# Transposes of x and h: from TensorE and ScalarE to transposing DMAs issued by SyncE

## The reference, cut to what matters

```python
xn = _layernorm(x, axis=-1)
s = _L0_attn_ref(xn, ...)          # causal convolution over l, 128 taps for each of 256 channels, plus xn * D
g = _silu(_L0_ffn_ref(xn, w_gate, w_up, w_down))
return x + s * g

# _L0_ffn_ref: fp4_linear quantises both operands in blocks of 16 along the last dim to the grid
# 0, .5, 1, 1.5, 2, 3, 4, 6 times (largest of the block)/6, and multiplies
gate = fp4_linear(x, w_gate); y = fp4_linear(x, w_up)      # 256 -> 704, each
h = jax.nn.silu(gate) * y
return fp4_linear(h, w_down)                               # 704 -> 256
```

## Time and profile before

| | |
|---|---|
| median of three executions | 586.62 us |
| the profiled execution | 586.48 us, of which its span is 584.7 us |
| TensorE matmuls, weight loads | 473.7 us (4956), 331.3 us (4956) |
| GpSimd | 198.4 us (302) |
| DMA | 70.80 MB in 101186 packets, 121 GB/s on average |

### The profile page before, as it was taken

The page is one execution under the profiler, slowest core; times in us unless marked ns, Lnnn a source line. Parts: engine busy times, 40 slices in busy tenths (PEclk is TensorE's granted clock), DMA queues, the critical chain, the costliest instruction groups (busy, mean ns, idle before and its releaser), DMA issues.

```text
span 584.7 us, 13233 instructions
## 1 busy us (share of the span) xinstructions
PE 473.7 (81%) x4956; PEld 331.3 (57%) x4956; DVE 544.3 (93%) x689; ACT 407.2 (70%) x568; POOL 198.4 (34%) x302
## 2 busy tenths in 40 slices
PE   0000356668999999999999999999999999998965
PEld 0000234225555567777777777777777777765654
DVE  6999999989999999999999999999999999998884
ACT  6972866889988876767676767676767666664552
POOL 1094000474555551111111111333333333137870
PEclk9999957989999999999999999999999999999998
DMA  5990012225222335353534353535354535339978
GB/s 173 349 281 1 1 36 90 91 27 163 91 91 91 109 83 159 102 146 108 149 105 142 112 147 103 144 111 146 104 143 114 144 107 148 110 59 154 172 104 132
DMA packets 101186, 70.80 MB, mean 121 GB/s; under 512 B 8848, under 2 KB 100752, under 8 KB 101008
## 3 DMA queue, kind: packets, MB, share of 16 engines
q1 hardware_dynamic: 93072, 61.94, 35.8%
q0 software_dynamic: 8064, 8.13, 9.5%
HBM read 61.28 MB, written 16.91 MB: 134 GB/s over the span
## 4 chain that ended last, share of the span: by engine, by line
PE 57%; DVE 24%; issue 9%; POOL 6%; ACT 3%; DMA 0%; SPq 0%; DVEq 0%; POOLq 0%; ACTq 0%
PE ps L1224 27%; PE ps L1242 10%; PE ps L1244 5%; PE ps L1233 5%; PE ps L1257 4%; PE ps L1261 4%; DVE wgu L944 4%; DVE work L857 2%; DVE sm L799 2%; POOL gbuf L516 2%; DVE work L883 2%; PE ps L1212 2%; DVE work L852 2%; DVE xh L919 1%; DVE xh L912 1%
## 5 line engine op out<-in xcount | busy, mean ns | idle before, releaser
L1224 PE MATMUL ps<-wgu,work 128*128 128x512 f16 (+1 forms) x1152 | 242.7, 366 | 17.1 <-DVE work L883 15.9
L1224 PEld LDWEIGHTS ps<-wgu,work 128*128 128x128 f16 x1152 | 109.9, 99 | 128.0 <-issue 17.5
L615 ACT ACTIVATE work<-ps,con 128x704 f32<-128x704 f32 x64 | 54.2, 847 | 95.1 <-PE ps L1224 95.0
L1242 PE MATMUL ps<-wdh,work 128*128 128x256 f16 x704 | 87.9, 274 | 5.5 <-ACT gbuf L619 4.7
L610 ACT COPY work<-ps 128x1408 f16<-128x1408 f16 x64 | 84.7, 1325 | 2.1 <-PE ps L1233 1.9
L852 DVE SCALAR_TENSOR_TENSOR work<-work 128x960 f32<-128x960 bf16 (+2 forms) x67 | 71.8, 1110 | 1.6 <-ACT work L630 1.5
L1242 PEld LDWEIGHTS ps<-wdh,work 128*128 128x128 f16 x704 | 65.4, 98 | 13.4 <-issue 5.3
L516 POOL TENSOR_TENSOR gbuf<-gbuf,xh 128x256 f32<-128x256 f32 (+1 forms) x42 | 41.0, 1048 | 92.0 <-DVE work L865 77.8
L857 DVE SCALAR_TENSOR_TENSOR work<-work 128x1920 f16<-128x1920 bf16 (+3 forms) x36 | 69.7, 1936 | 1.2
L818 DVE TENSOR_TENSOR work<-work,ps 128x960 f32<-128x960 f32 (+2 forms) x63 | 68.4, 1126 | 1.1
L630 ACT ACTIVATE work<-work 128x960 bf16<-128x960 f32 (+2 forms) x67 | 61.8, 960 | 9.3 <-DVE work L818 8.7
(11 more groups left out here) (153 smaller groups left out, 675.1 us busy)
## 6 DMA issues: line engine op xcount, KB each, us to landing
work<-kpad SPq DMA_DIRECT2D x64, 512.0 KB, 3.8
work<-L_attn_u SPq DMA_DIRECT2D x33, 256.0 KB, 3.0
gbuf<-u_rev SPq DMA_DIRECT2D x4, 2048.0 KB, 18.6
out<-gbuf POOLq DMA_DIRECT2D x7, 1024.0 KB, 9.5
out<-L_attn_u SPq DMA_DIRECT2D x1, 768.0 KB, 5.5
out<-gbuf POOLq DMA_DIRECT2D x1, 768.0 KB, 8.1
work<-L_ffn_w_down SPq DMA_DIRECT2D x1, 704.0 KB, 6.6
work<-L_ffn_w_gate SPq DMA_DIRECT2D x1, 640.0 KB, 4.7
```

The source lines that it names most:

```text
L1224: last = T.matmul(p_gu[:, a:b], xT[par][:, t, c, :], wgu[:, part, c % 2, a:b], start=(n == 0), stop=(n == len(todo) - 1))
L1242: T.matmul(dst, hT[t][:, c, :], wdh[:, c, :], start=(c == 0), stop=False)
```

## The change

The 256 + 682 transposes of TensorE for x and for all h tiles but the last two, and ScalarE's copies of them, are gone. In their place SyncE issues `dma_start_transpose` from SBUF to SBUF: one for each pair of x (128 x 1024 f16, 256 KB) and one for each tile of h (128 x 1408 f16, 352 KB). The last two tiles keep the old way. SyncE's queue is written out step by step without a loop: in each step x of pair it+1, then the even tile of h, then `load_x`, then the first `load_t`, then the odd tile of h, then the other `load_t`s. `load_x` stood first before.

```diff
+            def x_transpose(p):
+                sp.wait_ge(x_hl, p * 2 + 2)
+                after(sp, gu_p, p * 2 - 2)
+                sp.dma_start_transpose(xT[p % 2].rearrange("p t c k -> p (t c) k"),
+                                       xhl[p % 2].rearrange("p t c -> p (t c)")).then_inc(x_td[p % 2], 16)
+            def h_transpose(n):
+                sp.wait_ge(hl_v, n // 2 + 1)
+                after(sp, dn_p, n - 1)
+                sp.dma_start_transpose(hT[n % 2], hilo[n // 2 % 2][:, n % 2, :]).then_inc(h_td[n % 2], 16)
+            x_transpose(0)
+            sp.wait_ge(k_all, 1)
+            x_transpose(1)
+            for it in range(NP + 1):
+                if 1 <= it < NP - 1:
+                    x_transpose(it + 1)
+                if it >= 2:
+                    h_transpose(it * 2 - 4)
+                if it < NP - 3:
+                    load_x(it + 3, (it + 1) % 2)
+                if it == 2:
+                    store_filter()
+                if it < S_CONV:
+                    copy_input(it)
+                if it == S_CONV:
+                    load_t(1, 1)
+                tiles = [n for n in range(2 * groups_before(it) + 2, 2 * groups_before(it + 1) + 2) if n < H // 4]
+                for n in tiles[:1]:
+                    load_t(n, n % 2)
+                if it >= 2:
+                    h_transpose(it * 2 - 3)
+                for n in tiles[1:]:
+                    load_t(n, n % 2)
...
 # ScalarE: x_copy gone, h_copy only for the last two tiles. VectorE: x_parts and h_parts
 # wait for the DMAs that read the buffers. TensorE:
             def gate_up(m, t, par, first):
                 if first is not None:
-                    pe.wait_ge(x_tc, first)
+                    pe.wait_ge(x_td[par], (first + 1 - par) * 8)
...
             def down(n, t, dst=None):
-                pe.wait_ge(hT_a, n + 1)
+                pe.wait_ge(*((h_td[t], (n - t) * 8 + 16) if n < NT - 2 else (hT_a, n - (NT - 3))))
...
-                if td:
-                    pe.wait_ge(hl_v, it - 1)
-                    h_transpose(it * 2 - 4, 0, par, copied=min(it + 1, NP))
-                if x:
-                    x_transpose(it + 1, 1 - par)
-                if td:
-                    h_transpose(it * 2 - 3, 1, par, copied=it + 2 if x else None)
```

More of the change, by code:

```diff
@@ L145, in build @@
         rs_p, fl_p = (ps[:, 3584 + NC * i:3584 + NC * i + NC] for i in range(2))
-        p_xT = ps[:, 1536:2048].bitcast(F16).rearrange("p (t c k) -> p t c k", t=2, c=4)
         yv = xh[:, :, :, :, :].rearrange("p q a t c -> p (q a t c)").bitcast(F32).rearrange(
@@ L216, in build @@
         x_hl = sem("x_hl")
-        x_tp = sem("x_tp")
-        x_tc = sem("x_tc")
+        x_td = [sem(f"x_td{i}") for i in range(2)]
+        h_td = [sem(f"h_td{i}") for i in range(2)]
         t_in = [sem(f"t_in{i}") for i in range(2)]
@@ L424, in copy_input @@
                 sp.dma_start(out[i:i + 1, 0:rows], u[i:i + 1, 0:rows]).then_inc(o_in, 16)
-            for it in range(PEEL):
-                load_x(it + 3, (it + 1) % 2)
+            def x_transpose(p):
[7 more added lines that the diff above has]
+                sp.dma_start_transpose(hT[n % 2], hilo[n // 2 % 2][:, n % 2, :]).then_inc(h_td[n % 2], 16)
@@ L428, in _ @@
+            x_transpose(0)
[8 more added lines that the diff above has]
+                    load_x(it + 3, (it + 1) % 2)
                 if it == 2:
                     store_filter()
[L430 to L447, removed]
-                    load_t(n, n % 2)
@@ L449, in _ @@
-            for n in range(2 * groups_before(NP - 3) + 2, H // 4):
-                load_t(n, n % 2)
+                if it < S_CONV:
[4 more added lines that the diff above has]
+                for n in tiles[:1]:
+                    load_t(n, n % 2)
+                if it >= 2:
+                    h_transpose(it * 2 - 3)
@@ L451, in _ @@
+                for n in tiles[1:]:
+                    load_t(n, n % 2)
+                if it == S_CONV - 1:
+                    sp.wait_ge(k_pad, 32)
+                    sp.wait_ge(k_dram, 16 * 16)
+                    sp.wait_ge(w_ca, 13)
+                    load_t(0, 0)
             for n in range(2):
@@ L600, in x_norm @@
                 ins.then_inc(x_n, 1)
[L602 to L605, removed]
             def h_copy(n, par, src=p_hT):
-                act.wait_ge(hT_p, n + 1)
-                after(act, dn_p, n - 1)
+                act.wait_ge(hT_p, n - (NT - 3))
+                act.wait_ge(dn_p, n - 1)
                 nc.scalar.copy(hT[par], src).then_inc(hT_a, 1)
@@ L643, in y_copy, with step @@
                                      scale=con[:, C_CONV:C_CONV + 1]).then_inc(cv_e, 1)
-            def step(it, par, x, xt, xn, gu, ch, td, a2=False, cv=0, c0=None, td1=True, first=True):
-                if td:
-                    h_copy(it * 2 - 4, 0)
+            def step(it, par, x, xn, gu, ch, td, a2=False, cv=0, c0=None, td1=True, first=True):
                 if a2 and first:
@@ L659, in step @@
                     silu_out(it * 2 - 5, 1, 1 - par)
-                if xt:
-                    x_copy(it + 1, 1 - par)
                 if cv:
@@ L667, in step @@
                     silu_gate(it * 2 + 1)
-                if td:
-                    h_copy(it * 2 - 3, 1)
                 if a2:
@@ L738, in _ @@
             weights_out(range(6, 8))
-            x_copy(0, 0)
             act.wait_ge(w_g, 3)
@@ L748, in _ @@
             weights_out(range(11, 13))
-            x_copy(1, 1)
             for it in range(PEEL):
-                step(it, it % 2, True, it >= 1, True, True, it >= 1, it >= 2, a2=True, td1=it >= 3, first=it >= 1)
+                step(it, it % 2, True, True, True, it >= 1, it >= 2, a2=True, td1=it >= 3, first=it >= 1)
                 if it == 1:
@@ L756, in _ @@
                 for par in range(2):
-                    step(q * 2 + (PEEL + par), par, True, True, True, True, True, True, a2=True)
+                    step(q * 2 + (PEEL + par), par, True, True, True, True, True, a2=True)
             act.wait_ge(con_ok, 1)
@@ L760, in _ @@
                 for par in range(2):
-                    step(q * 2 + (S_CONV + par), par, True, True, True, True, True, True, cv=2 - par, c0=q * 3 + 2 * par)
+                    step(q * 2 + (S_CONV + par), par, True, True, True, True, True, cv=2 - par, c0=q * 3 + 2 * par)
             for it in range(S_TAIL, NP - 2):
[L763 to L766, removed]
+                step(it, it % 2, True, it < NP - 3, True, True, True, cv=groups_of(it), c0=groups_before(it))
+            step(NP - 2, 0, False, False, True, True, True)
+            step(NP - 1, 1, False, False, True, True, True)
+            step(NP, 0, False, False, False, True, True)
             silu_out(NT - 3, 1, 0)
@@ L861, in x_parts @@
                 dve.wait_ge(x_r, p + 1)
-                after(dve, x_tp, p - 1)
+                after(dve, x_td[par], (p - par) * 8)
                 for part, scale in enumerate((shi, slo)):
@@ L886, in h_parts @@
                 own.settle()
-                after(dve, hT_p, p * 2 - 2)
+                after(dve, h_td[0], p * 16 - 16)
+                after(dve, h_td[1], p * 16 - 16)
                 t0, t1 = only[0], only[-1] + 1
@@ L1226, in gate_up, with h_transpose @@
                 last.then_inc(gu_p, 1)
[L1228 to L1231, removed]
+            def h_transpose(n, t, par, dst):
                 for c in range(NC11):
@@ L1262, in conv, with step @@
                 last.then_inc(cv_h, 1)
-            def step(it, par, x, gu, td, cv=0):
-                if td:
-                    pe.wait_ge(hl_v, it - 1)
-                    h_transpose(it * 2 - 4, 0, par, copied=min(it + 1, NP))
+            def step(it, par, gu, td, cv=0):
                 if gu:
                     gate_up(it * 2, 0, par, it + 1)
-                if x:
-                    x_transpose(it + 1, 1 - par)
                 if cv:
@@ L1288, in step @@
                     conv(groups_before(it) + 1, 1)
-            x_transpose(0, 0)
             pe.wait_ge(w_ca, 8)
@@ L1305, in _ @@
             transposed_down(4)
-            x_transpose(1, 1)
             gate_up(1, 1, 0, None)
@@ L1309, in _ @@
             for it in range(1, NP - 1):
-                step(it, it % 2, True, True, it >= 2, groups_of(it) if it >= S_CONV else 0)
-            step(NP - 1, 1, False, True, True)
-            step(NP, 0, False, False, True)
+                step(it, it % 2, True, it >= 2, groups_of(it) if it >= S_CONV else 0)
+            step(NP - 1, 1, True, True)
+            step(NP, 0, False, True)
             down(NT - 3, 1)
```

## The result

The changed kernel takes 614.48 us (median of 4 runs, 612.14 to 616.2) against 587.18 us for the kernel before in the same runs. The ratio is 1.0455, with a 95% interval of 1.0432 to 1.0478: slower by 27 us, where 580 was forecast. The profiled execution took 613.09 us with a span of 611.2.

What follows compares the result with a forecast made beforehand. VectorE's own 14.34 us was taken to bound the steps, with TensorE adding 0.61 us to every second one in the convolution stage. 586.5 - 6.1 - 1.5 + 1.0 = 579.9, say 580 us; range 575 to 650.

Steps and rivals of the forecast that it cites:

- The bound of the convolution stage: Convolution stage: TensorE adds 0.61 us to every second step; removing it saves 6.1 us, then VectorE's 14.34 us bounds.
- rival C: Whole kernel: nothing measurable, gain offset by a costlier start and TensorE's lower clock, 585 to 588 us; chance 0.13.
- The 0.8 us of `h_parts`' waits: VectorE: waits of `h_parts` for the transposes that free its buffer, 0.8 us in all, counted as gone.
- SyncE's issuing: SyncE's queue: each transposing DMA takes 1 to 2.5 us to issue, at most 9.0 of 14.34 us a step.
- Rival A: SyncE's queue: transposing DMAs worked off block by block become the bound, about 850 us at 0.72 a block; chance 0.24.
- The engines' time: DMA engines: transposes add 3.3 us a step by bytes, or 7.1 by packets; the first was taken.
- what hides them is the pipeline's slack: Each step: each h tile has about 13 us to land, about three times the 3.8 us in which 512 KB land.
- Rival B: Convolution stage: the filter's loads come late, 1 to 2 us lost in all 20 steps, 600 to 620 us; chance 0.20.
- The prediction's own sign of being wrong: Whole kernel: the prediction is wrong at its root if a transposing DMA takes over 5 us.
- The start: Before the first `gate_up`: x of pair 0 takes 3.0 to 4.5 us in place of 2.3; 1.0 us loss taken.
- the convolution's end: Where the convolution ends: the last `y_copy` comes earlier relative to VectorE by 0 to 2 us; 0.7 us gain taken.

Runs made afterwards that it cites:

- x_only: The changed kernel with x alone by transposing DMA, in all steps, and h on TensorE: 581.53 us, ratio 0.9905 to the kernel before.
- no_acc: The changed kernel with GpSimd's accumulating DMAs left out except the last one: 588.61 us, ratio 1.0005 to the kernel before.
- plain: The changed kernel with each transposing DMA replaced by a plain DMA of the same bytes in rows of 2816 or 2048 bytes: 587.21 us, ratio 0.9999.
- plain256: The changed kernel with each transposing DMA replaced by a plain DMA of as many bytes in pieces of 256 bytes: 594.55 us, ratio 1.0124.
- conv_even: The changed kernel with only the even h tile of steps 8 to 27 by transposing DMA, all else on TensorE: 582.10 us, ratio 0.9908.

## Why the prediction was wrong

**The bound of the convolution stage** was right. 0.61 us for two steps was TensorE's, VectorE's 14.34 came next, and x_only gets 6.0 of 6.1 us. In the changed kernel 0.4 arrived. The change itself took nearly all the rest: five steps longer by 0.82 us, from a clock that falls behind the gaps it opened, 4.1 us, and 0.06 us a step of VectorE, 1.3, with the second wait in front of `h_parts`. I had put the clock in rival C, in the steps before this stage. The 0.8 us of `h_parts`' waits that I counted as gone did not come: it waits 0.8 us in all for transposing DMAs up to 520 us.

**SyncE's issuing** was right, at the lower end: 1.24 us for x in the median and from 1.27 for h, whose median of 1.82 has waits in it, against 1 to 2.5 forecast. Rival A, work by the block in order, did not happen: 11 blocks landed in 4.5 us in the median. The 1309 ns for one block that the Trainium skill gives ("VectorE: DVE Perf Modes", The three transpose paths) thus does not multiply by blocks. The estimate of 2.3 us of issuing for h, from the push command for each tile in "DMA: Bandwidth & Descriptors" of the Trainium skill, is above the 1.27 measured.

**The engines' time** was mis-sized. I took 3.3 us a step, by bytes, and kept 7.1, by packets of 256 bytes at 29.4 ns. The runs show the second: 31 ns a packet. That transposing DMAs are as fast as regular ones ("Advanced Engine Details and Errata", X-Bar Transpose, in the Trainium skill) is not borne out here. Against plain ones of the same bytes in long rows the engines' share in two steps was 96.5% to 64.1%, against plain pieces of 256 bytes a packet took 31 to 23 ns, and beside accumulating DMAs 60 to 20.

**The step that failed** is "what hides them is the pipeline's slack": 13 us for each h tile, "about three times the 3.8 us". The 3.8 us was the landing time of plain loads in the convolution stage, used for a stretch in which GpSimd's DMAs keep the engines 0.94 full. There a transposing DMA took 19.1 us, and the slack was gone. Rival B looked at these steps and dismissed them by tile 60 and its wait of 4.08 us. The late tiles were those before it, first of all in step 31, with 9.68 us. As this stretch comes last, nothing behind it could make up for it: 20.9 of the 26.6 us, and with either kind of DMA left out the same stretch took 63.6 to 66.7 us, so it takes both. The prediction's own sign of being wrong, a transposing DMA of over 5 us, would not have shown this as a median over the run, which is 4.4.

**Near rival B by luck.** The 614.48 us lie in its 600 to 620, but not for its reasons. B wanted late loads of the filter in even steps and 1 to 2 us lost in each of 20 steps. TensorE's waits for these loads are 1.3 us in all and the stage is no longer than before.

**The odd tile of step 2** was a second use of the same slack: the order of SyncE's queue in that step puts 10.4 us of issuing in front of it, which stood in the earlier trace rows as 11.52. It costs 4.7 us.

**The start** was right in kind: the first `gate_up` begins at 89.05 us in place of 87.30, but step 1 only 0.2 later, for 1.0 forecast. That is one execution: of the eight kernels whose profiled execution has x of pair 0 by DMA, three have step 1 at 109.1 to 109.2 and five at 110.1 to 110.6, where the granted clock stayed at 0.50 for longer and the 18 products of the first `gate_up` took 6.2 us and more in place of 5.2 to 5.5. At the convolution's end step 29 is 0.6 us shorter, for 0.7 forecast, and by the forecast's mechanism: the last `y_copy` comes 0.46 us behind VectorE's first instruction of the step in place of 1.20.

## What to carry to other kernels

Price a DMA that is to replace compute in each stage by what else is on the DMA engines there, in packets and not bytes, and above all in the last stage, where lateness is not made up. Move only as much work off an engine as brings it under the next bound: here x alone, one set of transposes of three, is worth the whole gain, and all three cost the clock and the engines' room. If a change opens gaps on TensorE, look at the granted clock of the products behind them: here it fell behind gaps of 1.97 us in four steps and not behind one of 1.98. And read landing times by stage, since a median over the run can hide the stage that matters.

## What the runs showed of the hardware

- Transposing DMAs and accumulating DMAs of GpSimd slow each other: 3.5 us of landing for the one alone (no_acc), 10.5 for the other alone, 19.1 and 24.0 together, with fewer bytes moved in 28 us (4.1 MB) than by the accumulating ones alone (4.5). Plain pieces of the same size leave the latter at 11.5.
- Plain DMAs of 352 KB from SBUF to SBUF in rows of 2816 bytes land in 3.6 us, in pieces of 256 bytes in 5.0, transposing ones in 4.5 (medians over the run of plain, plain256 and the changed kernel).
- A step of VectorE in a loop, with waits for values worked out in registers, takes up to 0.11 us longer than one written out with constants (14.41 against 14.30 in conv_even, 14.31 in the loop of x_only), about 15 instructions in each.
- TensorE's granted clock fell from 1.00 to 0.50 behind idle gaps of 1.97 us, and 18 products took 5.41 us in place of 3.73; 16 products of no use in the gap kept it at 1.00.
